# A Mamba block and a six-layer local-attention transformer on one core: V projected per tile, instead of V and output weights folded into one matrix per head

## The chip, the cores and the metric

One NeuronCore of one Trainium2 chip runs one launch. The metric is device time in microseconds (us), the median of a few executions. The kernel before takes 3925.72 us in the median of three (3923.69 to 3927.97).

## What is computed

The input is x, four sequences of 1024 tokens with 128 features, in float32. It goes through a bidirectional Mamba block and then through six transformer layers. The change lies in the attention of these layers; cut to that:

```python
x = x + ffn_ref(layernorm(x))        # the six layers below
for i in range(6):
    x = attn_layer(shift_tokens(x)) + x
    x = ffn_layer(shift_tokens(x)) + x

def attn_layer(x, Wqkv, qs, ksc, Wo):          # 16 heads of 64
    q, k, v = split(x @ Wqkv)                  # each 1024 wide
    q = rotary(l2norm(q) * qs); k = rotary(l2norm(k) * ksc)
    # windows of 32 queries see their own 32 keys and the 32 before
    sim = 8.0 * einsum('bhwie,bhwje->bhwij', q, k2)
    out = einsum('bhwij,bhwje->bhwie', softmax(mask(sim)), v2)
    return out @ Wo
```

## The kernel before

The Mamba block runs first, to about 1120 us. The transformer then works on tiles of 128 tokens (4 windows): 32 tiles a layer, 192 in all, and on chunks of 4 tiles (512 tokens) for the feed-forward part, 48 in all. Activations lie features on partitions (`xa`, `xb`).

A tile passes these stages. `round` (ACT) and `rest` (POOL) split x into a high and a low part; `project0` and `project1` (PE, L1043) multiply it by the weights of q and of k, 3 matmuls of 128x512 for each of two banks (high by high, low by high, high by low), so 12 a tile. ACT squares, DVE and POOL apply rotary tables and norms, `head_turn0..3` (PE, L1054) transpose q and k, four transposes each, and ACT copies them out (L1230). `score` (L1078, L1093) makes 64 small matmuls (16 heads, 4 windows; 64 rows of the array, 32 weight columns, 64 keys streamed) on top of two for the mask. `find_max` (DVE), `exponent` (ACT), `sum_probs` and `invert_sum` (DVE), `normalise_probs` (POOL, L1550) are the softmax, and `turn_probs` (DVE, L1414) transposes the probabilities in blocks of 32x32, which leaves the keys of each window on its own 32 partitions.

V is never formed. Once a layer `fold0` and `fold1` (PE, L1023) multiply each head's V weights by its output weights to a 128x128 matrix, which ACT copies to `w_vo` (`copy_folded`, L1190). Per tile `row_turn` (L1065) transposes x itself, once as it is and once 32 tokens back, `copy_rows` (ACT, L1237) copies both, `mix` (L1105) weights these rows with the probabilities of all 16 heads (8 matmuls of 32 rows by 128 columns, 512 streamed; the windows' four 32-row groups of the array side by side, each into a bank of its own), ACT copies the four banks (`copy_mixed0..3`, L1255), and `output` (L1116) sums over the 16 heads with `w_vo`:

```python
for place_h in range(HEADS):
    last = pe.matmul(bank[:, 0:P], w_vo[:, l % 2, head_at(place_h), :], mixed[:, odd, place_h, :],
                     start=place_h == 0, stop=place_h == HEADS - 1)
```

`add_output` (DVE) adds it to x. The feed-forward stages are `mean`, `variance`, `gate0..2`, `value0..2` (L1141) and `ff_output` (L1154).

Each engine runs its stages in an order written out in a table (`PE_ORDER`, `ACT_ORDER`, `DVE_ORDER`, `POOL_ORDER`): an entry (lag, which, name) stands for the stage of tile `which` of the chunk `lag` rounds back, and `sequence` unrolls it over the 48 chunks. `engine_sequences` puts in the stages that come once a layer. An engine waits on semaphores at the head of a stage, and everything behind it in the table waits too. Four PSUM banks (`turn_banks`) are taken in turn by the stages whose results are copied out; a stage waits until the reader of the bank's last use is done. SP issues weight loads only, when `copy_rows` of certain tiles is done.

## Time and profile before

| | us |
|---|---|
| median of 3 runs | 3925.72 (3923.69 to 3927.97) |
| span of the profiled execution | 3921.5 |
| PE busy | 3707.5 (95%) |
| DVE busy | 3319.6 (85%) |
| POOL busy | 3241.5 (83%) |
| ACT busy | 2915.4 (74%) |

The span is the time from the first to the last instruction of one profiled execution; that execution's own device time is not recorded separately, and its span stands 4.2 us under the median of the runs. PE is TensorE, PEld its weight loads, which run beside its matmuls. A matmul in float32 is recorded as two, each with a weight load; one in fp32r, and a transpose, as one. Busy time is a union: overlapping records count once, so a group's busy time over its number of stages is the price of a stage, while its mean ns holds the latency too.

### The profile page before, as it was taken

To read this page: it belongs to the slowest core of one execution; us is meant where nothing else is said; L and a number is where in the kernel's file an instruction comes from. 1 tells how busy PE (TensorE), PEld (TensorE's weight loads), DVE (VectorE), ACT (ScalarE), POOL (GpSimd) and SP (SyncE) were. 2 spreads that over 40 slices of the span, in tenths; PEclk is the share of its full clock that TensorE was granted. 3 is DMA by queue.
4 is the path that set the end of the run, shared out by engine and by line. 5 is a ranking of instruction groups with operands and counts; after the bars stand their busy time and mean duration, and the time that the engine had idled before them with its cause. 6 is when DMAs were issued, how large, how long until landed. Compare 5 with 4: busy or idle time off the path is not lost.

```text
span 3921.5 us, 110568 instructions
## 1 busy us (share of the span) xinstructions
PE 3707.5 (95%) x43392; PEld 2518.5 (64%) x43392; DVE 3319.6 (85%) x3407; ACT 2915.4 (74%) x6890; POOL 3241.5 (83%) x2370
## 2 busy tenths in 40 slices
PE   7889989988789999999999999999999999999997
PEld 2333333333377777777777777777767777777775
DVE  4999999999688888888888887888878888788885
ACT  7555445553388887888888887888878888888885
POOL 3888888888698888888888888888888888888883
PEclk8999998998899999999999999999999999999999
DMA  1221222212100000000000000000000000000001
GB/s 68 73 76 70 76 71 75 76 71 83 50 16 2 16 3 2 17 2 16 3 6 13 2 16 2 6 13 3 16 2 6 13 2 16 2 6 2 2 3 44
DMA packets 31567, 102.12 MB, mean 26 GB/s; under 512 B 4676, under 2 KB 6600, under 8 KB 30928
## 3 DMA queue, kind: packets, MB, share of 16 engines
q1 hardware_dynamic: 31056, 95.05, 7.0%
q8 instruction: 352, 5.77, 0.6%
q14 instruction: 159, 1.30, 0.1%
HBM read 90.32 MB, written 4.72 MB: 24 GB/s over the span
## 4 chain that ended last, share of the span: by engine, by line
PE 68%; issue 2%; ACT 2%; DVE 0%; POOL 0%; POOLq 0%; ACTq 0%; DVEq 0%
PE ps L1116 17%; PE ps L1043 13%; PE ps L1105 9%; PE ps L1054 8%; PE ps L1093 7%; PE ps L1141 5%; PE ps L1154 3%; PE ps L1078 2%; PE ps L1065 1%; PE ps L1123 1%; PE ps L1129 1%; ACT prob L1246 0%; PE ps L1023 0%; ACT mixed L1255 0%; ACT w_qk L1175 0%
## 5 line engine op out<-in xcount | busy, mean ns | idle before, releaser
L1521 POOL TENSOR_TENSOR resid<-resid,sq 128x1024 f32<-128x1024 f32 x384 | 910.8, 2377 | 3.4 <-DVE sq L1376 2.9
L626 POOL TENSOR_TENSOR read<-state,c_row 128x1024 f32<-128x1024 f32 x256 | 719.8, 2831 | 153.9 <-DVE state L588 84.9
L1543 POOL TENSOR_TENSOR resid<-resid,rnorm 128x1024 f32<-128x1024 f32 x384 | 725.0, 1904 | 18.1 <-POOL rnorm L1535 0.4
L1116 PE MATMUL ps<-mixed,w_vo 128*128 128x128 f32 x6144 | 720.7, 276 | 3.0 <-ACT mixed L1255 2.8
L1116 PEld LDWEIGHTS ps<-mixed,w_vo 128*128 128x128 f32 x6144 | 711.5, 193 | 12.9 <-issue 4.6
L1043 PE MATMUL ps<-w_qk,xs_parts 128*128 128x512 f32 x2304 | 634.6, 411 | 35.4 <-issue 18.1
L1246 ACT ACTIVATE prob<-ps,stat 128x64 f32<-128x64 f32 x3072 | 653.5, 385 | 0.7 <-DVE stat L1396 0.5
L1376 DVE TENSOR_TENSOR sq<-ps,rope_l 128x1024 f32<-128x1024 f32 x384 | 462.4, 1204 | 101.5 <-ACT sq L1208 101.2
L393 PE MATMUL mamba_ps<-read,ident 128*128 128x512 f32 x1024 | 509.6, 638 | 15.4 <-POOL read L626 15.4
L1389 DVE TENSOR_TENSOR resid<-ps,rope_l 128x1024 f32<-128x1024 f32 x384 | 464.3, 1209 | 66.9 <-ACT sq L1208 59.7
L1043 PEld LDWEIGHTS ps<-w_qk,xs_parts 128*128 128x128 f32 x2304 | 412.4, 191 | 148.6 <-issue 73.8
L1550 POOL TENSOR_TENSOR prob<-prob,stat 128x1024 f32<-128x1024 f32 x192 | 366.1, 1907 | 165.3 <-DVE stat L1407 165.3
L1208 ACT ACTIVATE sq<-ps 128x1024 f32<-128x1024 f32 x384 | 395.7, 1030 | 141.3 <-PE ps L1043 111.8
L1255 ACT COPY mixed<-ps 128x512 f32<-128x512 f32 x768 | 399.5, 602 | 111.8 <-PE ps L1105 111.7
L522 ACT ACTIVATE decay<-dt,neg_a 128x1024 f32<-128x1024 f32 x256 | 280.4, 1143 | 268.1 <-DVE state L588 212.6
L1353 DVE TENSOR_REDUCE ssq<-sq 128x16 f32<-128x1024 f32 x384 | 465.7, 1213 | 6.1 <-ACT sq L1208 1.7
L1054 PE MATMUL ps<-ident,resid 128*128 128x128 f32 x3072 | 414.4, 275 | 13.7 <-ACT w_vo L1190 13.1
L588 DVE TENSOR_TENSOR_SCAN state<-decay,mamba_ps 128x1024 f32<-128x1024 f32 x176 | 396.3, 2274 | 3.7
L1054 PEld LDWEIGHTS ps<-ident,resid 128*128 128x128 f32 x3072 | 351.3, 141 | 74.6 <-issue 60.8
L1105 PE MATMUL ps<-prob_t,rows 32*128 32x512 f32 x3072 | 385.2, 613 | 4.1 <-DVE xb L1424 1.6
L393 PEld LDWEIGHTS mamba_ps<-read,ident 128*128 128x128 f32 x1024 | 196.9, 202 | 283.5 <-issue 247.1
L1230 ACT COPY q_t<-ps 128x512 f32<-128x512 f32 x384 | 230.9, 602 | 127.0 <-PE ps L1054 125.0
(138 smaller groups left out, 5676.8 us busy)
## 6 DMA issues: line engine op xcount, KB each, us to landing
c_row<-c_rows SPq DMA_DIRECT2D x128, 512.0 KB, 3.6
w_stage<-w_qk_hbm SPq DMA_DIRECT2D x12, 512.0 KB, 4.7
vo_stage<-w_v_hbm SPq DMA_DIRECT2D x6, 512.0 KB, 3.7
vo_stage<-w_o_hbm SPq DMA_DIRECT2D x6, 512.0 KB, 4.6
xn<-x_hbm SPq DMA_DIRECT2D x4, 512.0 KB, 6.6
kept<-resid SPq DMA_DIRECT2D x8, 256.0 KB, 4.4
resid<-kept SPq DMA_DIRECT2D x8, 256.0 KB, 4.0
out_hbm<-resid SPq DMA_DIRECT2D x8, 256.0 KB, 2.0
```

The source lines that it names most:

```text
L393: last = pe.matmul(y_ps[h][:, c, :], ident[:, :], read[:, h, g % 2, cols(c)], start=False, stop=n == LAST)
L626: pool.tensor_tensor(read[:, h, g % 2, :], state[:, h, g % 2, :], c_row[:, g % C_AHEAD, :], ALU.mult).then_inc(done[f"rd{h}"], 1)
L1043: last = pe.matmul(ps[:, A + c, :], xs_parts[:, odd, xpart, :], w_qk[:, wpart, cols], start=k == 0, stop=k == 2)
L1054: last = pe.transpose(bank[:, j * P:(j + 1) * P], qk[:, tile % 2, col:col + P], ident[:, :])
L1105: last = pe.matmul(banks[w], rows[rows_w, tile % 2, own, :], prob_t[rows_w, tile % 2, :, own, :], start=own == 0, stop=own == 1)
L1116: last = pe.matmul(bank[:, 0:P], w_vo[:, l % 2, head_at(place_h), :], mixed[:, odd, place_h, :], start=place_h == 0, stop=place_h == HEADS ...
L1246: last = act.activation(prob[:, tile % 2, place_h, :], score_ps[:, place_h, :], ACT.Exp, bias=stat[:, tile % 2, 0, place_h:place_h + 1])
L1353: dve.tensor_reduce(ssq[:, tile % 2, part * HEADS:(part + 1) * HEADS, 0], sq[:, 0, :].rearrange("p (h d) -> p h d", d=HEAD_DIM), AX_X, ALU ...
L1376: dve.tensor_tensor(sq[:, 1 + part, :].rearrange("p (h s d) -> p h s d", s=2, d=HEAD_DIM // 2), swapped, table(part, 1, tile).rearrange("p ...
L1389: dve.tensor_tensor(qk[:, tile % 2, part * INNER:(part + 1) * INNER].rearrange("p (h d) -> p h d", d=HEAD_DIM), heads_ps.rearrange("p (h d ...
L1521: pool.tensor_tensor(qk[:, tile % 2, cols], qk[:, tile % 2, cols], sq[:, 1 + part, :], ALU.add).then_inc(done[f"rotated{part}"], 1)
L1543: pool.tensor_tensor(heads, heads, norms, ALU.mult).then_inc(done[f"normed{part}"], 1)
```

## The change

V is computed for each tile: `projv` makes 6 matmuls of the form of `project`, `copy_v0` and `copy_v1` (ACT) bring it to `values`, and two DMAs on SP (`vshift`) write the rows of 32 tokens back beside it. `turn_probs` transposes into a single `prob_t`, and eight DMAs on SP (`pmove`, 64 KB each) move its rows to `by_key`, in which the 64 keys that a window sees lie on 64 partitions. `mix` becomes 64 small matmuls (8 pairs of heads, 2 kinds of window, 2 halves of the rows, 2 heads of a pair): 64 rows by 64 weight columns, 32 queries streamed. ACT copies two banks instead of four, and `output` sums over 8 pairs of heads with the plain output weights. `fold`, `copy_folded`, `row_turn` and `copy_rows` go. The V weights are split once a layer (`high_v` on ACT, `low_v` on POOL, 128x1024 each). `xs_parts` has 4 slots instead of 2. All five tables of the transformer are new; in the Mamba part semaphores are merged.

```diff
-    (2, 2, "head_turn2"), (2, 3, "head_turn0"), (2, 3, "head_turn2"), (2, 3, "head_turn3"), (2, 2, "score"),
+    (4, 1, "project1"), (6, None, "variance"), (4, 0, "head_turn1"), (5, 3, "score"), (5, 1, "mix"), (5, 3, "projv"),
...
+SP_ORDER = [
+    (1, 1, "vshift"), (1, 0, "pmove"), (1, 1, "pmove"), (1, 2, "vshift"), (1, 3, "vshift"), (1, 2, "pmove"),
+    (1, 3, "pmove"), (0, 0, "vshift")]
...
+        insert_after(act, ("copy_v1", last), ("high_v", l))
+        insert_at(pool, (name, last + ahead), ("low_v", l))
...
-    several = {"mix": WINDOWS, "fold0": 2, "fold1": 2}
+    several = {"projv": 2, "mix": 2}
...
+            def shift_values(tile):
...
+                after(sp, ("copy_v0", tile), ("copy_v1", tile))
+                if tile >= 2:
+                    after(sp, ("mix", tile - 2))
...
+                sp.dma_start(v_back[WINDOW:P, odd], v[0:P - WINDOW, odd]).then_inc(v_shifted[odd], 16)
+                sp.dma_start(v_back[0:WINDOW, odd], v[P - WINDOW:P, before]).then_inc(v_shifted[odd], 16)
...
+            def move_probs(tile):
+                odd = tile % 2
+                after(sp, ("turn_probs", tile))
+                if tile >= 2:
+                    after(sp, ("mix", tile - 2))
+                for w in range(WINDOWS):
+                    of = prob_t[w * WINDOW:(w + 1) * WINDOW]
+                    for own in range(2):
+                        first = w // 2 * 64 + own * WINDOW
+                        sp.dma_start(by_key[first:first + WINDOW, odd, w % 2], of[:, own]).then_inc(probs_moved[odd], 16)
...
+            def project_v(tile):
...
+                after(pe, ("rest", tile))
...
+                for c in range(2):
+                    for k, (xpart, wpart) in enumerate([(0, 0), (1, 0), (0, 1)]):
+                        last = pe.matmul(banks[c], xs_parts[:, tile % X_RING, xpart, :], w_v[:, wpart, c * BANK:(c + 1) * BANK],
+                                         start=k == 0, stop=k == 2)
...
             def mix(tile):
-                after(pe, ("turn_probs", tile), ("copy_rows", tile))
-                banks = [turn_free("mix", tile, w) for w in range(WINDOWS)]
-                for own in range(2):
-                    for w in range(WINDOWS):
-                        rows_w = slice(w * WINDOW, (w + 1) * WINDOW)
-                        last = pe.matmul(banks[w], rows[rows_w, tile % 2, own, :], prob_t[rows_w, tile % 2, :, own, :],
-                                         start=own == 0, stop=own == 1)
+                after(pe, ("copy_v0", tile), ("copy_v1", tile))
+                shifted_back(pe, tile)
+                moved(pe, tile)
+                banks = [turn_free("mix", tile, r) for r in range(2)]
+                for a in range(PAIRS):
+                    for second, of in enumerate((v_back, v)):
+                        to = slice(64 * a + WINDOW * second, 64 * a + WINDOW * second + WINDOW)
+                        for r in range(2):
+                            keys = slice(64 * r, 64 * r + 64)
+                            for h in range(2):
+                                head = 2 * a + h
+                                last = pe.matmul(banks[r][64 * h:64 * h + 64, to], of[keys, odd, head * HEAD_DIM:(head + 1) * HEAD_DIM],
+                                                 by_key[keys, odd, second, h * PAIRS + a, :], start=True, stop=True)
...
-                for place_h in range(HEADS):
-                    last = pe.matmul(bank[:, 0:P], w_vo[:, l % 2, head_at(place_h), :], mixed[:, odd, place_h, :],
-                                     start=place_h == 0, stop=place_h == HEADS - 1)
+                for a in range(PAIRS):
+                    last = pe.matmul(bank[:, 0:P], w_o[:, l % 2, a, :], mixed[:, odd, a, :], start=a == 0, stop=a == PAIRS - 1)
...
+                    act.copy(v[:, tile % 2, c * BANK:(c + 1) * BANK], turn_bank("projv", tile, c)).then_inc(done[f"copy_v{c}"], 1)
...
-                if tile >= 2:
-                    after(dve, ("mix", tile - 2))
-                dve.transpose(prob_t[:, tile % 2].rearrange("p h o n -> p (h o n)"),
-                              prob[:, tile % 2].rearrange("p h k -> p (h k)")).then_inc(done["turn_probs"], 1)
+                if tile:
+                    moved(dve, tile - 1)
+                dve.transpose(prob_t.rearrange("p o h n -> p h o n"),
+                              prob[:, tile % 2].rearrange("p h (o n) -> p h o n", o=2)).then_inc(done["turn_probs"], 1)
```

Three places of the new order. First PE in the middle of the transformer. Before, a stretch from a `score` to the second `mix` behind it (`ps<-prob_t,rows` is `mix`, `ps<-mixed,w_vo` is `output`, `ps<-ident,xa` is `row_turn`):

```order
L1093 MATMUL ps<-k_t,q_t 32x64 x64
L1105 MATMUL ps<-prob_t,rows 128x512 x8
L1043 MATMUL ps<-w_qk,xs_parts 128x512 x6
L1129 MATMUL ps<-work_ff,ones_mean 128x512
L1065 MATMUL ps<-ident,xa 128x128 x2
L1116 MATMUL ps<-mixed,w_vo 128x128 x16
L1054 MATMUL ps<-ident,resid 128x128 x4
L1043 MATMUL ps<-w_qk,xs_parts 128x512 x6
L1105 MATMUL ps<-prob_t,rows 128x512 x8
```

Now, from the mix of the second tile of a chunk to that of the third (`ps<-by_key,values` is `mix`, `ps<-w_v,xs_parts` is `projv`, the first of them that of the fourth tile, `ps<-hidden,w` is `ff_output`):

```order
L1133 MATMUL ps<-by_key,values 64x32 x64
L1076 MATMUL ps<-w_v,xs_parts 128x512 x6
L1086 MATMUL ps<-ident,resid 128x128 x4
L1063 MATMUL ps<-w_qk,xs_parts 128x512 x6
L1086 MATMUL ps<-ident,resid 128x128 x4
L1181 MATMUL ps<-hidden,w 128x512 x3
L1086 MATMUL ps<-ident,resid 128x128 x4
L1076 MATMUL ps<-w_v,xs_parts 128x512 x6
L1063 MATMUL ps<-w_qk,xs_parts 128x512 x6
L1133 MATMUL ps<-by_key,values 64x32 x64
L1100 MATMUL ps<-sight_hidden,sight_rows 128x512 x2
```

Between the fourth tile's `projv` and the third tile's `mix` stand seven stages: three of 4 transposes, two `project`, one `ff_output` and one `projv`.

Second ACT, at the copies of the fourth tile's V (`values<-ps`), around the same place of the program:

```order
L1283 COPY mixed<-ps 128x8x64 x2
L1265 COPY values<-ps 128x512
L1222 CAST xs_parts<-xa 128x128
L1265 COPY values<-ps 128x512
L1253 COPY q_t<-ps 128x512
L1231 ACTIVATE sq<-ps 128x1024
L1239 ACTIVATE rnorm<-floored 128x32
```

The two copies follow the two of `mixed`, with a cast between them.

Third SP, which had nothing to issue per tile before (`values<-values` is `vshift`, `by_key<-prob_t` is `pmove`):

```order
L995 DMA values<-values 96x1024 [waits mix,copy_v1,copy_v0]
L996 DMA values<-values 32x1024
L995 DMA values<-values 96x1024 [waits mix,copy_v1,copy_v0]
L996 DMA values<-values 32x1024
L1007 DMA by_key<-prob_t 32x512 [waits mix,turn_probs]
L1007 DMA by_key<-prob_t 32x512 x7
```

The moves of the third tile's probabilities stand behind the shifts of the fourth tile's V, which wait for that tile's copies.

## Rows read from the trace of the kernel before

**Rows 1.** The page: span, busy time of each engine.

```profile
span 3921.5 us, 110568 instructions
...
PE 3707.5 (95%) x43392; PEld 2518.5 (64%) x43392; DVE 3319.6 (85%) x3407; ACT 2915.4 (74%) x6890; POOL 3241.5 (83%) x2370
```

**Rows 2.** The view by stretch; columns of its second line.

```profile
core 0: us, PE busy (x) PEld busy (x) DVE busy (x) ACT busy (x) POOL busy (x), PEclk, DMA share, GB/s
0.00:1120.00 1120.00, 968.37 (x2737) 406.01 (x2738) 987.43 (x668) 596.12 (x743) 878.65 (x365) 0.92 0.20 70
1120.00:1200.00 80.00, 76.46 (x1237) 60.09 (x1236) 65.84 (x77) 66.58 (x176) 71.38 (x59) 0.98 0.05 16
1200.00:3800.00 2600.00, 2561.64 (x38205) 1979.20 (x38205) 2191.70 (x2568) 2177.82 (x5784) 2235.91 (x1906) 1.00 0.02 7
3800.00:3921.00 121.00, 101.07 (x1218) 73.20 (x1218) 74.65 (x97) 74.87 (x191) 55.56 (x42) 0.96 0.11 36
```

**Rows 3.** Waits of PE from 1200 to 3800 us: total, times, longest.

```profile
PE ps L1043 <- issue: 18.1, 7, 3.6
PE ps L1054 <- ACT w_vo L1190: 13.1, 10, 1.3
PE ps L1093 <- issue: 3.3, 10, 0.6
PE ps L1065 <- ACT mixed L1255: 1.2, 5, 0.2
```

**Rows 4.** Groups of PE by form: busy, mean ns | idle.

```profile
L1116 PE MATMUL ps<-mixed,w_vo 128*128 128x128 f32 x6144 | 720.7, 276 | 3.0 <-ACT mixed L1255 2.8
L1043 PE MATMUL ps<-w_qk,xs_parts 128*128 128x512 f32 x2304 | 634.6, 411 | 35.4 <-issue 18.1 <-DVE resid L1389 7.8 <-DVE sq L1376 7.8
...
L1054 PE MATMUL ps<-ident,resid 128*128 128x128 f32 x3072 | 414.4, 275 | 13.7 <-ACT w_vo L1190 13.1
L1105 PE MATMUL ps<-prob_t,rows 32*128 32x512 f32 x3072 | 385.2, 613 | 4.1 <-DVE xb L1424 1.6 <-ACT hidden L1297 0.9
...
L1154 PE MATMUL ps<-hidden,w 128*128 128x512 f32 x192 | 91.7, 601 | 3.8 <-DVE hidden L1438 3.8
...
L1065 PE MATMUL ps<-ident,xa 128*128 128x128 f32 x384 | 75.9, 279 | 1.3 <-ACT mixed L1255 1.2
...
L1154 PE MATMUL ps<-hidden,w 85*128 85x512 f32 x96 | 49.4, 595 | 0.0
...
L1023 PE MATMUL ps<-vo_stage 64*128 64x128 f32 x192 | 13.7, 284 | 0.0
```

**Rows 5.** Timeline of PE: start, us, what.

```profile
1606.44 2.00 PE L1105 MATMUL ps<-prob_t,rows 32*128 32x512 f32 x16
...
1608.69 1.48 PE L1093 MATMUL ps<-k_t,q_t 64*32 64x64 f32 x128
...
1230.11 3.73 PE L1116 MATMUL ps<-mixed,w_vo 128*128 128x128 f32 x32
```

**Rows 6.** Timeline of PE's weight loads in the same score.

```profile
1608.69 1.32 PEld L1093 LDWEIGHTS ps<-k_t,q_t 64*32 64x32 f32 x128 [0.23 <-issue]
```

**Rows 7.** Groups of ACT by form.

```profile
L1255 ACT COPY mixed<-ps 128x512 f32<-128x512 f32 x768 | 399.5, 602 | 111.8 <-PE ps L1105 111.7
...
L1237 ACT COPY rows<-ps 128x256 f32<-128x256 f32 x192 | 77.1, 402 | 0.0
...
L1175 ACT CAST w_qk<-w_stage 128x1024 fp32r<-128x1024 f32 x12 | 13.3, 1104 | 0.0
L1190 ACT COPY w_vo<-ps 128x512 f32<-128x512 f32 x24 | 13.0, 607 | 0.0
```

**Rows 8.** Groups of POOL by form, 1120 to 3921 us.

```profile
L1550 POOL TENSOR_TENSOR prob<-prob,stat 128x1024 f32<-128x1024 f32 x189 | 360.4, 1907 | 165.3 <-DVE stat L1407 165.3
...
L1481 POOL TENSOR_TENSOR w_qk<-w_stage,w_qk 128x1024 fp32r<-128x1024 f32 x10 | 23.6, 2363 | 0.0
```

**Rows 9.** Groups of DVE by form, 1120 to 3921 us.

```profile
L1414 DVE STREAM_TRANSPOSE prob_t<-prob 128x1024 f32<-128x1024 f32 x189 | 234.3, 1240 | 73.2 <-POOL prob L1550 71.8
```

**Rows 10.** Timeline of SP's queue: start, us, DMAs issued.

```profile
4.84 0.81 SPq L272 DMA_DIRECT2D packed<-packed_hbm  x1
...
49.53 1.28 SPq L281 DMA_DIRECT2D c_row<-c_rows  x3
```

**Rows 11.** DMA issues: KB each, median us to landing.

```profile
out_hbm<-resid SPq DMA_DIRECT2D x8, 256.0 KB, 2.0
...
c_rows<-x_dbl SPq DMA_DIRECT2D x8, 64.0 KB, 3.1
...
head_scale<-head_scale_hbm SPq DMA_DIRECT2D x6, 64.0 KB, 4.7
```

260 lines of the change are left out of this document (130 added, 130 removed), and 40 rows, old and new, of tables (ACT_ORDER, DVE_ORDER, PE_ORDER, POOL_ORDER).

## The prediction

> **What bounds the kernel now.** I read the view by stretch first [rows 2]. The Mamba part, to about 1120 us, is not touched by the change (its semaphores are merged, its order stands), so its time stays. In the 2600 us from 1200 on PE is busy for 2561.64, or 98.5%, at a granted clock of 1.00, which is the upper of TensorE's two levels, 2.4 GHz; POOL has 86%, DVE and ACT 84%. The waits of PE in that stretch [rows 3] come to 36 us in all. So the transformer is paid in PE time alone, and every microsecond taken from PE is worth one, until another engine is reached. Over the transformer PE is busy 76.46 + 2561.64 + 101.07 = 2739 us, POOL 2363, DVE 2332, ACT 2319, in a stretch of 3921 - 1120 = 2801 us; PE is idle for 62 us of it, 26 of them outside the middle stretch, where the pipeline fills and drains.
>
> The sum is made against the span of the profiled execution, 3921.5 us [rows 1]. The median of the runs lies 4.2 us above it, and differences are applied to the median.
>
> **The change, part by part, on PE.** Prices of a stage are the busy time of its group over the number of stages.
> - `row_turn` goes: -75.9 us [rows 4].
> - `fold` goes: -13.7 us [rows 4]. With it goes the wait of `head_turn` for the copy of its result, -13.1 us [rows 3].
> - `output` has 8 matmuls of the same form instead of 16: half of 720.7 us, -360.4 [rows 4]. A timeline row shows the stage whole: 3.73 us for 32 records [rows 5].
> - `projv` adds 6 matmuls a tile of the form that `project` has 12 of: half of 634.6 us, +317.3 [rows 4].
> - `mix` today costs 385.2 us, 2.0 us a tile [rows 4, 5]. Its successor, 64 matmuls of 64 rows by 64 weight columns with 32 streamed, is in no row. The nearest one is `score`, also 64 matmuls, of 64 rows by 32 weight columns with 64 streamed: 1.48 us [rows 5]. The new mix streams half as much through places of the array twice as large, so 4 fit side by side instead of 8, and its weight loads are twice as wide. If the number of matmuls or the streaming sets the pace, it costs what `score` does, 1.48 us. If the loads do, it costs up to twice that, 2.96: in `score` the loads fill 1.32 of the 1.48 us [rows 6], so I can't exclude them as the pace. I take 2.0 us, a little under the middle and the price of the stage that it replaces; that makes -1 us, with ends of -101 and +183.
>
> Together -75.9 - 13.7 - 360.4 + 317.3 - 1.2 = -134 us of PE work, to 2605, and -13 us of waiting.
>
> **The other engines.** ACT: `copy_rows` goes (-77.1), the copies of `w_vo` go (-13.0), two copies of `mixed` are replaced by two of V in the same form at 602 ns (0), and `high_v` adds six casts at 1104 ns (+7) [rows 7]: 2236 us, 86% of the new PE work. POOL: `low_v`, six times 2363 ns (+14) [rows 8]: 2377, 91%. DVE: `turn_probs` keeps its size at 1240 ns, but writes in pieces of 32 [rows 9]; below, nothing would be saved; above, twice the price would be +238 us. I take no change, since it turns blocks of 32x32 before and after: 2332, 90%. These costs lie beside PE, which still has the most work. But the cover gets thin: POOL waits 165.3 us in front of `normalise_probs` alone [rows 8], which is a chain and not spare time. I add 20 us of new PE idle time for it.
>
> **SP and the DMAs.** Ten DMAs a tile are new. Three issued in a row take 1.28 us, so 0.43 each; one single issue took 0.81 [rows 10]. Ten are 4.3 us of SP in a tile's 13.6 (2605/192): no bound. What they move, 1 MB a tile, is about 77 GB/s; the Mamba part runs at 70 GB/s with the DMA engines 20% busy [rows 2]. The delay matters. The landing of 64 KB took 3.1 us with one source and 4.7 with another, and 256 KB out took 2.0 [rows 11]. The new mix of a tile waits for its eight moves, which wait for `turn_probs`, and the next `turn_probs` waits for the landing as well, since `prob_t` is single. The tightest place is the one that the orders show: the moves of a chunk's third tile stand on SP behind the shifts of the fourth tile's V. From the end of that tile's `projv` the chain is two copies and a cast on ACT (about 1.5 us), ten issues (4.3) and a landing (3.1 to 4.7): 8.9 to 10.5 us. On PE seven stages lie between: three of 4 transposes (414.4/768 = 0.54 each), three of 6 matmuls (1.65 each) and `ff_output` ((91.7 + 49.4)/48 = 2.9), 9.5 us [rows 4]. So it is just covered at the short landing, and I cost it at nothing. If the cover goes, PE stands in `mix` with `score` and everything else queued behind it. At the end of the program one chain isn't covered: eight issues and a landing, 3.4 + 3.1 = 7 us.
>
> **The sum.** 3925.7 - 134 - 13 + 20 + 7 = 3806 us, 3.1% less.
>
> **Rivals.**
> 1. *The weight loads set the pace of `mix`.* For it: they are twice as wide, and there are 128 per tile. Against: in `score` they run partly beside one another. At 2.96 us a tile it is (2.96 - 2.0) x 192 = +184 us, 3990: slower than before. It decides from 3925.7 - 3806 = 120 us, that is 0.62 us a tile, so from 2.62 us on.
> 2. *`mix` is as cheap as `score`.* For it: same number of matmuls, half the streaming. 0.52 x 192 = -100, less what POOL gives back, since its 2377 us are then 95% of 2505: 3706 to 3726, about 3715.
> 3. *PE waits in `mix` for the moved probabilities.* With the long landing 10.5 - 9.5 = 1.0 us once in each of 48 chunks: +48, 3854. Were each issue to take 0.81, it would be 1.5 + 8.1 + 4.7 - 9.5 = 4.8 us a chunk, +230, 4036, but the shorter issue has three in a row behind it.
> 4. *POOL or DVE becomes the bound.* Their work is unchanged while PE's shrinks by 5%. If half of the 134 us is lost again in their chains: +67, 3873. A dearer `turn_probs` would lead here as well.
> 5. *The change doesn't do what it says* on PE: excluded by the orders, which show `output` at 8, `projv` at 6 and `mix` at 64 matmuls.
>
> **Rule and trace.** Beside rival 1: the loads of `score`, 64 of 32 columns on each half of the rows, are done within 1.32 us [rows 6], 21 ns a load. The Trainium skill (TensorE: Matmul & The Clock Gate, section LDWEIGHTS) puts a load at its columns over 1.2 GHz, 27 ns for 32 and 53 ns for 64. By that rule the new mix would take 64 x 53 = 3.4 us a tile on each half, and the sum would come out at about 4075 us, estimated from that page. The trace is on the faster side of that rule, so it moves no chance. The Trainium skill (TensorEngine Tiling (Array Packing), section Instruction Overhead) gives each matmul about 60 cycles however little it streams; at 2.4 GHz that is 25 ns, for 64 matmuls 1.6 us, an estimate from that page that would bring the sum to about 3730 us. The 64 matmuls of `score` took 1.48 us, 23 ns each, which agrees with it, and speaks for rival 2.
>
> **How the numbers follow.** A difference of 0.2%, 8 us, is about what a measurement of this kernel can tell from none. The forecast has 0.42, rival 1 0.13, rival 2 0.18, rival 3 0.13 and rival 4 0.11; 0.03 is left for something not seen. Faster: the forecast, rivals 2 to 4 but for their far ends (0.02), together 0.82. Slower: rival 1 nearly whole, the far end of rival 3 and half of the unseen, 0.14. The rest, 0.04, is same. The range goes from rival 2, 3715, over rivals 3 and 4 to the point where `mix` costs 2.7 us, 3940; it leaves out the slow half of rival 1 and a little at the cheap end, under 2 in 10.
>
> **What would show it.** PE's group of `mix` over 192: 2.0 us (1.5 is rival 2, above 2.6 rival 1). `output` near 360 us, `projv` near 317, PE busy in all near 3707 - 134 = 3574. Waits of PE in the middle of the transformer: some 30 to 50 us, with nothing on a DMA of `by_key`; over 50 us there is rival 3, on ACT's, DVE's or POOL's results rival 4. `turn_probs` at 1240 ns. A mix above 2.6 us, or a wait on the moved probabilities of more than 2.5 us a chunk, makes the prediction wrong.

## The result, and the profile after

The changed kernel takes 4511.1 us (median of 4 runs, 4508.91 to 4514.13) against 3926.84 us of the kernel before, measured on the same chip: a ratio of 1.149, 95% interval 1.1473 to 1.1506. That is 584 us slower where 120 us less was forecast, and far outside the range. The page of the profiled execution, to read against [rows 1]; the two lines at the end are the clock by slices and the DMA queue that carries instructions:

```profile
span 4512.3 us, 150478 instructions
...
PE 3887.2 (86%) x62400; PEld 2789.0 (62%) x62400; DVE 3324.7 (74%) x3407; ACT 2951.2 (65%) x6772; POOL 3262.0 (72%) x2376
...
PEclk8999999989889899989989999998999889999987
...
q8 instruction: 500, 8.19, 0.8%
```

The work of DVE and POOL is what it was, as forecast; ACT has 2951.2 us where the forecast had 2832 (the last part comes back to it). PE has 3887.2 us of work where the forecast had 3574 (+313), and is idle for 4512.3 - 3887.2 = 625 us where it had 3802 - 3574 = 228 (+397); 3802 is the forecast of 3806, less the 4 us by which the span stands under the median. The two together are the whole miss of 710 us of the span. By stretch [rows 2], the Mamba part is unchanged and the transformer is different everywhere:

```profile
0.00:1120.00 1120.00, 962.26 (x2886) 401.70 (x2887) 985.16 (x664) 590.66 (x720) 878.48 (x361) 0.93 0.22 72
...
1200.00:3800.00 2600.00, 2256.24 (x46140) 1845.47 (x46138) 1811.89 (x2118) 1834.35 (x4693) 1862.10 (x1575) 0.91 0.25 66
```

PE is busy for 87% of the stretch instead of 98.5%, and its granted clock is 0.91 instead of 1.00. PE's groups by form, to read against [rows 4]:

```profile
L1063 PE MATMUL ps<-w_qk,xs_parts 128*128 128x512 f32 x2304 | 668.6, 428 | 29.4 <-issue 8.9 <-DVE resid L1417 8.2 <-POOL w_qk L1509 6.7
...
L1086 PE MATMUL ps<-ident,resid 128*128 128x128 f32 x3072 | 480.6, 298 | 12.2 <-issue 6.2 <-POOL resid L1577 5.7
L1133 PE MATMUL ps<-by_key,values 64*64 64x32 f32 x24576 | 480.6, 230 | 341.1 <-issue 320.1 <-DMA by_key<-prob_t 16.9
L1076 PE MATMUL ps<-w_v,xs_parts 128*128 128x512 f32 x1152 | 388.4, 482 | 3.0 <-issue 3.0
L1144 PE MATMUL ps<-mixed,w_o 128*128 128x128 f32 x3072 | 370.0, 277 | 0.0
L1115 PE MATMUL ps<-k_t,q_t 64*32 64x64 f32 x23808 | 319.1, 231 | 78.0 <-issue 78.0
```

The idle time stands in two groups, `mix` (341.1) and `score` (78.0), and almost all of it is "issue": the profile names no engine and no transfer that PE waited for. The waits of the middle stretch [rows 3] say the same:

```profile
PE ps L1133 <- issue: 252.2, 156, 6.0
PE ps L1115 <- issue: 62.0, 53, 2.5
...
PE ps L1133 <- DMA by_key<-prob_t: 2.0, 2, 1.5
```

Not all of that is one thing. 44 of these stops, 49.3 us, stand at the head of the mix of a chunk's third tile, as here:

```profile
1257.31 5.17 SPq L1007 DMA_DIRECT2D by_key<-prob_t  x8
...
1264.19 1.61 PE L1133 MATMUL ps<-by_key,values 64*64 64x32 f32 x97 [1.45 <-issue]
```

The last of the eight moves is issued at 1261.9 us and lands 2.0 us later, and PE starts 0.3 us after that. Each of the 44 ends within 0.5 us of such a landing. They are waits for the moved probabilities that the profile files under "issue". With the 13.5 us that it puts down to the DMA at the same place in the other 4 chunks, all 48 chunks pay there, 62.8 us in all. The stops inside a stage are the larger part: 224 of them, 350 us, of which 266 in `mix` and 84 in both forms of `score`'s matmuls.

The timeline shows where in a stage PE stops. Two pieces, a score and the mix behind it, twice:

```profile
2017.06 1.48 PE L1115 MATMUL ps<-k_t,q_t 64*32 64x64 f32 x128
2018.57 1.55 PE L1133 MATMUL ps<-by_key,values 64*64 64x32 f32 x90
2021.64 1.08 PE L1133 MATMUL ps<-by_key,values 64*64 64x32 f32 x38 [1.51 <-issue]
...
2034.39 1.72 PE L1115 MATMUL ps<-k_t,q_t 64*32 64x64 f32 x128
2036.13 0.55 PE L1133 MATMUL ps<-by_key,values 64*64 64x32 f32 x22
2038.54 2.74 PE L1133 MATMUL ps<-by_key,values 64*64 64x32 f32 x106 [1.86 <-issue]
```

The stop is in the middle of a mix, once after 90 and once after 22 records, where no instruction waits for a semaphore: all of a mix's waits stand ahead of its first matmul. My reading was that PE is short of instructions. Counting supports it: a float32 matmul of this kernel leaves two records and each record has a weight load, so a mix issues 256 instructions, as a score does, where the old mix issued 32. The traces also show the fetches themselves, as packets of the queue that carries instructions: every one of the 224 stops inside a mix or a score of this kernel ends 1.2 to 1.7 us after such a packet has been moved. Run 4 below shows a row of them. The clock by stretch over the same place (stretch and its length, busy times of the five engines, clock, DMA share, GB/s):

```profile
2018.60:2021.60 3.00, 1.52 (x90) 1.41 (x91) 3.00 (x4) 1.54 (x2) 0.68 (x1) 1.00 0.02 5
2021.60:2026.50 4.90, 4.86 (x51) 4.07 (x51) 2.48 (x5) 1.66 (x3) 3.55 (x2) 0.65 0.02 5
2026.50:2031.00 4.50, 4.50 (x33) 4.08 (x32) 4.20 (x5) 4.24 (x13) 0.97 (x4) 1.00 0.23 56
...
2038.50:2044.00 5.50, 5.46 (x113) 4.71 (x113) 2.58 (x4) 1.07 (x2) 3.59 (x2) 0.55 0.02 4
```

Behind both stops the granted clock falls to 0.55 to 0.65, a mixture of full and half speed (2.4 and 1.2 GHz), for some 5 us in which PE is fully busy, and comes back. So these two stops cost twice: once themselves, and again in the work behind them.

The theories that the experiments had to tell apart: **B**, two stages of 256 instructions in a row use up PE's instructions faster than they come; **A**, the instructions come late because their transfers stand behind the changed kernel's 200 MB of new DMAs; **M**, the small matmuls themselves are slow, whatever stands around them.

### The profile page after: what moved, and what is told of

It reads as the page before. It is cut to its first block, busy times and chain, and to the rows that moved or that the text cites. A ratio compares the mean times of both kernels' runs of the same rounds, so it can differ in the third digit from the quotient of the medians.

```text
span 4512.3 us, 150478 instructions
## 1 busy us (share of the span) xinstructions
PE 3887.2 (86%) x62400; PEld 2789.0 (62%) x62400; DVE 3324.7 (74%) x3407; ACT 2951.2 (65%) x6772; POOL 3262.0 (72%) x2376
## 4 chain that ended last, share of the span: by engine, by line
PE 63%; issue 10%; POOL 2%; ACT 1%; SPq 1%; DMA 0%; DVE 0%; DVEq 0%; ACTq 0%; POOLq 0%
PE ps L1063 12%; PE ps L1133 10%; PE ps L1086 8%; PE ps L1076 8%; PE ps L1144 7%; PE ps L1115 7%; PE ps L1168 5%; PE ps L1181 3%; PE ps L1100 1%; PE ps L1150 1%; PE ps L1156 1%; SPq L1007 1%; POOL resid L1577 0%; POOL resid L1555 0%; ACT prob L1274 0%
## 5 line engine op out<-in xcount | busy, mean ns | idle before, releaser
L625 POOL TENSOR_TENSOR read<-state,c_row 128x1024 f32<-128x1024 f32 x256 | 719.9, 2832 | 154.4 <-DVE state L587 85.0
L1133 PE MATMUL ps<-by_key,values 64*64 64x32 f32 x24576 | 480.6, 230 | 341.1 <-issue 320.1
L1063 PE MATMUL ps<-w_qk,xs_parts 128*128 128x512 f32 x2304 | 668.6, 428 | 29.4 <-issue 8.9
L1133 PEld LDWEIGHTS ps<-by_key,values 64*64 64x64 f32 x24576 | 448.1, 146 | 393.3 <-issue 383.5
L1063 PEld LDWEIGHTS ps<-w_qk,xs_parts 128*128 128x128 f32 x2304 | 454.2, 207 | 126.4 <-issue 34.8
L1563 POOL TENSOR_TENSOR newton<-floored,rnorm 128x32 f32<-128x32 f32 x192 | 49.0, 255 | 660.6 <-ACT rnorm L1241 660.3
L1283 ACT COPY mixed<-ps 128x512 f32<-128x512 f32 x384 | 207.3, 595 | 484.9 <-PE ps L1133 484.9
L1086 PEld LDWEIGHTS ps<-ident,resid 128*128 128x128 f32 x3072 | 415.2, 156 | 137.6 <-issue 64.1
L1086 PE MATMUL ps<-ident,resid 128*128 128x128 f32 x3072 | 480.6, 298 | 12.2 <-issue 6.2
L1115 PE MATMUL ps<-k_t,q_t 64*32 64x64 f32 (+1 forms) x24576 | 319.6, 231 | 84.2 <-issue 84.2
L1076 PE MATMUL ps<-w_v,xs_parts 128*128 128x512 f32 x1152 | 388.4, 482 | 3.0 <-issue 3.0
```

The source lines that it names most:

```text
L625: pool.tensor_tensor(read[:, h, g % 2, :], state[:, h, g % 2, :], c_row[:, g % C_AHEAD, :], ALU.mult).then_inc(done[f"rd{h}"], 1)
L1063: last = pe.matmul(ps[:, A + c, :], xs_parts[:, tile % X_RING, xpart, :], w_qk[:, wpart, cols], start=k == 0, stop=k == 2)
L1076: last = pe.matmul(banks[c], xs_parts[:, tile % X_RING, xpart, :], w_v[:, wpart, c * BANK:(c + 1) * BANK], start=k == 0, stop=k == 2)
L1086: last = pe.transpose(bank[:, j * P:(j + 1) * P], qk[:, tile % 2, col:col + P], ident[:, :])
L1115: last = pe.matmul(ps[w * WINDOW:(w + 1) * WINDOW, S + h, first:(a + 1) * 2 * WINDOW], q_t[rows_h, odd, a, w * WINDOW:(w + 1) * WINDOW], k ...
L1133: last = pe.matmul(banks[r][64 * h:64 * h + 64, to], of[keys, odd, head * HEAD_DIM:(head + 1) * HEAD_DIM], by_key[keys, odd, second, h * P ...
```

## The experiments

All ratios are against runs of the kernel before on the same chip, with 95% intervals. "Gaps" is the idle time on "issue" in `mix` and `score` together, by PE's groups, the waits at the head of a mix with it; "inside" is the time of the stops inside these stages, without those.

**1. No DMAs.** The ten moves of a tile are issued for the first two tiles only; later tiles mix stale probabilities and V.

```diff
             def move_probs(tile):
...
+                if tile >= 2:
+                    return
```

> The changed kernel, with the ten DMAs of a tile (shifts of V, moves of the probabilities) issued for the first two tiles only; all later tiles multiply stale probabilities and stale shifted V, so the output isn't the reference's. PE's order and instructions are the same. Theory A (instruction fetch waits behind these DMAs): the gaps inside mix vanish, the granted clock returns to 1.00 in the transformer, 3790 to 3850 us. Theory B (burst of instructions alone): gaps stay, over 4350 us.

4302.89 us, 1.0967 (1.0887 to 1.1048), in neither theory's range. Gaps 305 us instead of 398, clock 0.938 instead of 0.914.

```profile
L1137 PE MATMUL ps<-by_key,values 64*64 64x32 f32 x24576 | 450.2, 223 | 239.2 <-issue 229.7 <-DVE xa L1485 2.8 <-ACT k_t L1257 1.5
```

So 208 of the 584 us go with the DMAs, and 376 us are there without them: A is a part, and not the main one. In the profiles PE is idle for 103 us less and works 99.5 us less. The waits at the head of a mix, 66 us with those named as the DMA's, are gone, and the stops inside shrink from 350 to 308 us at nearly the same number (224 and 229).

**2. The DMAs alone.** The kernel before with ten DMAs a tile of the same sizes on SP, from SBUF to a scratch in HBM.

> The kernel before, with ten extra DMAs a tile on SP of the sizes of the change (384, 128 and eight of 64 KB), from a constant tile to a scratch in HBM, that nobody waits for but SP. PE's work is the same. Theory A: instructions arrive late behind them, gaps appear in score (one heavy stage a tile instead of two), 3980 to 4150 us. Theory B: no gaps, 3926 to 3940 us.

3932.94 us, 1.0027 (1.0011 to 1.0043). The score's gaps rise from 3.4 to 10.1 us, and that is all:

```profile
L1105 PE MATMUL ps<-k_t,q_t 64*32 64x64 f32 x23808 | 291.1, 226 | 10.3 <-issue 10.1
```

The same traffic costs some 10 us (0.27%) here and 208 in the changed kernel, where PE also waits for what is moved. (The destination differs too, HBM in place of SBUF, so the comparison isn't exact.)

**3. Twice the score, no DMAs.** The kernel before, each of score's matmuls given twice.

```diff
-                for a in range(PAIRS):
+                for a in list(range(PAIRS)) * 2:
```

> The kernel before, with the 64 matmuls of score issued twice in a row (scores doubled, so another output), which adds 256 records a tile right behind the 256 of score, and no DMA. PE's work grows by 1.3 to 1.5 us a tile, 250 to 290 us. Theory A: no gaps without data DMAs, 4180 to 4220 us. Theory B: gaps inside score as in the changed kernel, and a lower clock, 4350 to 4550 us.

4616.64 us, 1.1767 (1.1677 to 1.1857): +690 us for 192 x 1.48 = 284 us of matmuls, more than B's own range (4350 to 4550). A timeline row pair shows B with no DMA and no new form of matmul:

```profile
2013.71 1.83 PE L1093 MATMUL ps<-k_t,q_t 64*32 64x64 f32 x165
2017.14 1.12 PE L1093 MATMUL ps<-k_t,q_t 64*32 64x64 f32 x91 [1.60 <-issue]
```

The page gives the size of what is fetched. The queue of instructions has 544 packets instead of 352; the edit adds 24576 records and as many loads, and 49152 / 192 = 256 instructions a packet. 8.91 MB / 544 is 16 KB, so 64 bytes each. The Trainium skill (Perfetto Trace Analysis, section Per-instruction lifecycle, The 4-stage abstract model) calls instructions 64 bytes long, and the trace agrees.

**4. Four times the score,** to see the pace at which PE goes once its stock is used up.

> Kernel before with every tile's score made of its matmuls four times in a row into the same outputs (the same values are written four times; no transfer is added but the instructions themselves, no order moved). It puts 1024 instructions of PE, matmuls and weight loads, in a row. Theory of fetched instructions: after the instructions at hand are used up PE goes at the pace at which they come, so the last half of each stage shows a steady rate, one stop for each few hundred instructions: with 17 us of added stage at 1.83 us for 165 records gapless the stage would be 512 records in 6 us; by the theory it takes 8 to 12 us. The total is 4616 (score twice) plus 128 tiles times 2 layers... that is 384 tiles in all times 2 more scores of 2.3 to 4 us each: 6000 to 7500 us. Theory M: 512 records run at 1.48 us for 128 to the end, and the total is about 3926 plus 192 tiles times 3 scores times 1.48, 4780 us.

6301.35 us, 1.6066 (1.6028 to 1.6103). A score of this kernel:

```profile
2626.16 2.02 PE L1093 MATMUL ps<-k_t,q_t 64*32 64x64 f32 x183
2630.38 1.47 PE L1093 MATMUL ps<-k_t,q_t 64*32 64x64 f32 x128 [2.20 <-issue]
2633.85 2.04 PE L1093 MATMUL ps<-k_t,q_t 64*32 64x64 f32 x128 [2.00 <-issue]
2637.60 1.34 PE L1093 MATMUL ps<-k_t,q_t 64*32 64x64 f32 x73 [1.71 <-issue]
```

After 183 records the stage falls into a step: 128 records, that is 256 instructions, one packet, then a stop, and the starts are 3.47 and 3.75 us apart. So PE takes in one packet in 3.47 to 3.75 us and uses one up in 1.48 us of score or 2.07 us of mix. The stage took 12.8 us where 512 records at full pace take 5.9, a little over the 8 to 12 expected.

The view of the DMAs from 2620 to 2640 us, in 40 slices of 0.5 us, shows the packets (the 16 is one of another queue):

```profile
GB/s 0 0 0 0 0 0 0 0 16 0 0 0 0 0 0 33 0 0 0 0 0 0 33 0 0 0 0 0 0 33 0 0 0 0 0 0 0 33 0 0
...
q8 instruction: 4, 0.07, 1.5%
```

They begin at 2627.79, 2631.43, 2634.90 and 2638.70 us, and PE goes on 2.4 to 2.7 us after each of the first three. All 566 stops of this trace inside a score end 1.2 to 1.6 us after a packet has been moved. A packet itself is moved in 1.1 us on average and the DMA share of the stage is 0.02, so it is the delay of a fetch and not the rate of the DMA engines that makes the step of 3.5 us. This shows B directly, since no data DMAs were added.

**5. The same work, mixes moved away from scores.** In the changed kernel, three of the four mixes of a chunk, with their copies and `projv`, go behind a later `project0` in PE's and ACT's orders.

> The changed kernel, with three of the four mixes of a chunk moved behind the next project0 (their copies on ACT and the projv that depends on them with them), so that they no longer stand directly behind score. Theory A (PE runs out of instructions because their fetch waits behind SP's data DMAs, wherever the heavy stages stand): 4400 to 4530 us, little better than 4511. Theory B (two stages of 256 records each in a row want instructions faster than an undisturbed fetch brings them): three of four places are mended, so 4050 to 4200 us, and the idle time inside mix falls from 341 us to about 100.

4603.48 us, 1.1733 (1.1661 to 1.1806): slower, a miss for the total that B expected. The part that B is about went as it said: gaps fall from 398 to 166 us. But the edit by hand opened other waits, 97.6 us on ACT's copies in `mix` and 66.7 us on DVE in `project` the largest; over all of PE's groups the waits on ACT and DVE grow by some 265 us. With them the sum closes: PE is idle for 77 us more than in the changed kernel and works 8 us more. A gapless mix is seen here, next to what it costs:

```profile
2043.21 2.07 PE L1112 MATMUL ps<-by_key,values 64*64 64x32 f32 x128
...
L1112 PE MATMUL ps<-by_key,values 64*64 64x32 f32 x24576 | 467.0, 231 | 226.9 <-issue 119.3 <-ACT k_t L1232 97.6 <-DMA by_key<-prob_t 8.7
```

**6. Fewer instructions in the mix, same DMAs.** 32 matmuls of 64 columns in place of 64 of 32.

```diff
-                for a in range(PAIRS):
+                for a in range(0, PAIRS, 2):
...
-                                                  by_key[keys, odd, second, h * PAIRS + a, :], start=True, stop=True)
+                                                  by_key[keys, odd, second, h * PAIRS + a:h * PAIRS + a + 2, :], start=True, stop=True)
```

> The changed kernel with 32 matmuls in mix instead of 64, each streaming 64 columns instead of 32 (the weights of one head are used for two, so half of the heads' values are wrong): same columns streamed, same DMAs with the same bytes, half of the weight loads and half of the instructions. Theory B: gaps inside mix below 80 us, 3750 to 3900 us. Theory A: gaps stay above 200 us, above 4250 us.

4035.64 us, 1.0291 (1.0267 to 1.0315). The streaming and the bytes moved are unchanged and 475 of 584 us are gone. B had expected still more (3750 to 3900 us, gaps inside `mix` under 80):

```profile
L1133 PE MATMUL ps<-by_key,values 64*64 64x64 f32 x12288 | 250.2, 226 | 207.9 <-issue 173.3 <-DMA by_key<-prob_t 31.1
```

The run doesn't part B from M by itself, since the mix's own busy time fell by 230 us (480.6 to 250.2). The stops inside went from 350 to 194 us.

**7. The mix in bfloat16.** 128 instructions a mix instead of 256, and half the bytes in the moves. POOL writes the rounded probabilities to one buffer, and so waits for the last `turn_probs` too.

```diff
-    prob_t = sb("prob_t", [P, 2, HEADS, WINDOW])
-    by_key = sb("by_key", [P, 2, 2, HEADS, WINDOW])
+    prob_t = sb("prob_t", [P, 2, HEADS, WINDOW], BF16)
+    by_key = sb("by_key", [P, 2, 2, HEADS, WINDOW], BF16)
```

> The changed kernel with V, its shifted copy and the probabilities of mix in bf16 (rounded by the copies of V and by normalise_probs): every matmul of mix is one record with one weight load instead of two, so mix brings 128 instead of 256 instructions at the same count of 64 matmuls, and the moves carry half the bytes. Theory B (PE consumes instructions faster than they are fetched, decided by their number in a row): the gaps inside mix fall from 341 us to below 80, the clock is near 1.00, 3700 to 3850 us. Theory M (the small matmuls themselves, their weight loads or the array's tiles, hold PE up): the gaps stay near 300 us, 4300 us or more. Theory A (fetch behind data DMAs only): their number is unchanged and their bytes halved, 4300 to 4450 us.

3985.57 us, 1.016 (1.0133 to 1.0187), over B's range of 3700 to 3850. It is 50 us under the run before it, with half the bytes and 105 us less busy time in the mix (250.2 to 145.6), so the bytes matter little next to the instructions. PE has 3469.4 us of work, less than the kernel before, and the kernel is still slower: gaps are 247 us.

**8. Less work elsewhere, same small stages.** `projv` with its high parts only (2 matmuls, not 6; V is coarser), on the changed kernel and on run 7.

> The changed kernel, projv with the high parts alone (2 matmuls a tile instead of 6), mix untouched: less PE work by 190 to 210 us, the same 256 instructions of mix behind the 256 of score. Theory B with a supply that refills between heavy stages: the time that falls away was refill time, so the gaps inside mix grow and part of the 200 us is lost: 4350 to 4450 us. If supply weren't the limit, all of it would be gained: 4300 to 4320 us.

4354.0 us, 1.1103 (1.1077 to 1.1129).

> The kernel of the bf16 mix, and projv with the high parts alone (2 matmuls a tile instead of 6; V loses its low parts, which bf16 drops anyway). PE's work falls by another 190 to 210 us, below that of POOL, whose 2377 us in the transformer then bound. Theory B: 3600 to 3750 us, faster than both kernels. Theory A: over 4100 us.

3938.45 us, 1.0043 (1.0028 to 1.0058). The first lies in its range (4350 to 4450), the second is far over its own (3600 to 3750). Two thirds of the group of `projv` are 259 us in the changed kernel (of 388.4) and 220 in run 7 (of 329.9). Leaving them out was worth 157 in the one and 47 in the other. The gaps, which B had expected to grow in the first, fell in both (398 to 318, 247 to 206) and stayed the largest idle item; the busy time of `project` and of the transposes rose instead (668.6 to 711.0 and 480.6 to 503.2 in the first), and in the second a wait of 57 us for `by_key` came up.

**9. The lighter mix with the orders of run 5.**

> Changed kernel with the mix in bfloat16 (V, its shifted copies and the moved probabilities are rounded to bfloat16, one recorded matmul and weight load instead of two) and, in addition, the orders of PE and ScalarE moved so that three of four mixes of a chunk no longer stand right behind a score (mix and its copies go behind a later project). Theory of fetched instructions: the gaps for instructions, 153.6 us in mix and 93.5 in score when only the mix was in bfloat16, fall to a third or less as they did under the same move in float32 (295 to 119), and since less is issued at once the clock rises from .945; against it stand the waits that the move itself opened (some 200 us in the float32 case). Net: 3930 to 4050 us, with gaps for instructions in mix and score together under 100 us. Theory M (the small matmuls themselves): the gaps stay at 245 us together, and the total is over 4100 us.

4176.01 us, 1.0654 (1.063 to 1.0678). Again the gaps fell, 247 to 76 us, and the total missed: 190 us slower than run 7.

```profile
L1044 PE MATMUL ps<-w_qk,xs_parts 128*128 128x512 f32 x2304 | 648.5, 418 | 128.5 <-issue 47.5 <-DVE resid L1398 37.6 <-DVE sq L1385 36.8
...
L1114 PE MATMUL ps<-by_key,values 64*64 64x32 bf16 x12288 | 140.2, 182 | 143.3 <-ACT k_t L1234 97.5 <-issue 34.8 <-DMA by_key<-prob_t 9.4
```

The place of a stage can't be changed by hand for one cause alone; each time some 260 us of new waits on ACT and DVE took the place of the gaps.

**10. Score and mix both in bfloat16.** On top of run 7:

```diff
-    q_t = sb("q_t", [P, 2, PAIRS, P])
-    k_t = sb("k_t", [P, K_RING, PAIRS, P])
+    q_t = sb("q_t", [P, 2, PAIRS, P], BF16)
+    k_t = sb("k_t", [P, K_RING, PAIRS, P], BF16)
```

> Changed kernel with the mix and also the score in bfloat16 (V, its shifted copies, the moved probabilities, and q and k are rounded to bfloat16): 64 recorded matmuls instead of 128 in each of the two stages, so that both together issue what score alone issues in the kernel before; orders and all transfers stay (those of mix have half the bytes). Theory of fetched instructions: the gaps for instructions in score and mix, 247 us with only the mix in bfloat16, fall under 60 us; PE's busy time falls by another 100 to 170 us to about 3330. What the total does then tells whether the rest of the step from 3926 was bound by PE at all: if PE alone sets the pace, it is 3986 minus 190 gap minus 130 work, about 3670 us, and waits for transfers stay small; if, as the run with the lighter output showed (360 us less work on PE, total unchanged), the order of the transformer stands at some 3900 us through ScalarE, VectorE and POOL whatever PE has, it is 3850 to 3930 us with PE waiting for those engines by 200 us and more. Theory M (small matmuls are slow in themselves) leaves gaps of 150 us and more for instructions and a total over 3950 us.

3786.69 us, 0.9644 (0.9627 to 0.9662): faster than both kernels. Score and mix together now issue what score alone issued before. Its groups of the two stages:

```profile
L1135 PE MATMUL ps<-by_key,values 64*64 64x32 bf16 x12288 | 137.0, 181 | 171.8 <-DMA by_key<-prob_t 101.7 <-issue 62.7 <-DVE xa L1483 0.9
...
L1117 PE MATMUL ps<-k_t,q_t 64*32 64x64 bf16 x11904 | 133.6, 196 | 24.8 <-issue 24.8
```

The total lies between the two that were weighed (3670, and 3850 to 3930). Gaps are 87 us where under 60 were expected, but 49 of them stand at the head of a mix, just behind a landing of its probabilities; inside the stages 39 are left. The waits for the moved probabilities, my rival 3, are now the larger item: those 49 us and the 101.7 named as the DMA's.

**11. The same edit of q and k on the kernel before and on the changed one.**

> Kernel before with q and k rounded to bfloat16, so that score issues 64 recorded matmuls and 64 weight loads a tile instead of 128 each; nothing else is changed. It tells whether the gain seen with both stages in bfloat16 (3787 us) belongs to the lighter score or to the changed kernel's structure. If PE's work sets the pace of before, 1.48 us of score a tile becomes about 0.75 us: 192 times 0.75 us, 140 us less, about 3785 us, no different from the changed kernel with both light. If instead the transformer of before already stands at its other engines (as the run with the lighter output said, 360 us less on PE and no gain), it stays at 3900 to 3930 us, and then the changed kernel's structure, once its instructions are few, is worth about 3.5%.

3846.8 us, 0.9803 (0.9787 to 0.982), again between the two expected (3785, and 3900 to 3930).

> Changed kernel with q and k rounded to bfloat16 and the mix left in float32: score issues 64 matmuls and 64 weight loads, mix 128 of each, where the changed kernel has 128 and 128, the run with a bfloat16 mix 128 and 64, and the last run 64 and 64. Theory of fetched instructions: what counts is how many instructions stand in a row (score, then mix), so this one should be like the run with the light mix (3986 us) and far from the changed kernel (4511): 3980 to 4150 us, the transfers of mix having their full bytes; gaps for instructions 200 to 280 us, now nearly all in mix, under 30 us in score. If something in the mix itself (its matmuls of 32 columns in float32, or what they read) makes it slow, halving the score changes little: 4300 us or more.

4124.64 us, 1.0509 (1.0485 to 1.0532), gaps 224 us, nearly all in the mix, all as expected by B. Its timeline shows the stock from the other side: 64 and 127 records went through, and the last one had to wait.

```profile
2045.93 0.68 PE L1115 MATMUL ps<-k_t,q_t 64*32 64x64 bf16 x64
2046.72 2.06 PE L1133 MATMUL ps<-by_key,values 64*64 64x32 f32 x127
2051.25 0.19 PE L1133 MATMUL ps<-by_key,values 64*64 64x32 f32 x1 [2.47 <-issue]
```

These runs side by side, in instructions of score and mix in a row (matmul records and loads):

| kernel | score + mix | gaps, us | inside, us | waits for moved probabilities, us | total, us |
|---|---|---|---|---|---|
| changed | 256 + 256 | 398 | 350 | 66 | 4511 |
| changed, score light (11) | 128 + 256 | 224 | 163 | 124 | 4125 |
| changed, mix light (7) | 256 + 128 | 247 | 204 | 66 | 3986 |
| changed, both light (10) | 128 + 128 | 87 | 39 | 151 | 3787 |
| before | 256 + 32 | 3.4 | 4 | none | 3926 |
| before, score light (11) | 128 + 32 | 0 | 0 | none | 3847 |

The waits are those named as the DMA's, and those at the head of a mix under "issue" that end within 0.5 us of a landing of `by_key`. "Inside" counts both forms of the score's matmuls, "gaps" the larger one.

The stops inside follow the count. M falls: the same edit of the score, a stage that the change does not touch, takes 386 of the 584 us from the changed kernel and 79 from the kernel before, though the score's own busy time falls by nearly the same in both (204 and 177 us). At the same count runs 7 and 11 differ by 139 us; in the profiles that is PE's work (3469.4 against 3617.6), while its idle time differs by 10. The changed structure gains 60 us on the old one (3847 to 3787) once both stages are light, with a mix in float32 in the old one.

**12. Half of `output` taken away in the kernel before.** The product is held in the reduced float32 that TensorE takes in one record instead of two, with operands rounded more coarsely.

```diff
-    w_vo = sb("w_vo", [P, 2, HEADS, P])
+    w_vo = sb("w_vo", [P, 2, HEADS, P], F32R)
...
-    mixed = sb("mixed", [P, 2, HEADS, P])
+    mixed = sb("mixed", [P, 2, HEADS, P], F32R)
```

> Kernel before with one change: the product of the output projection (the folded weight of V and output, and the mixed values that it is multiplied with) is held in the reduced form of float32 that TensorE takes in one matmul instead of two, so its operands are rounded more coarsely than before. No order is moved. It takes 16 of 32 recorded matmuls (and as many weight loads) out of each tile's output, 720.7 us of PE by the rows of before, with 3.73 us for 32 recorded matmuls at one width. Theory of fetched instructions (PE stops where its instructions are used up faster than they come): the stage gets lighter in instructions, no new gap for instructions appears in score or mix, and PE's busy time falls by 360 (half of 720.7) to 540 us (a quarter left, if the single matmul is also faster a column). Then PE is no longer alone: POOL with 2363 us of work in the transformer's 2362 us of PE time cannot follow, so the total falls by less: 3550 to 3800 us. Theory that small matmuls themselves are what made the changed kernel slow (M) expects the same fall. A total above 3926 would say that something other than PE sets the transformer's pace already in the kernel before.

3918.44 us, 0.9993 (0.9978 to 1.0008). (The Mamba part, which had worked in `mixed`, works in other buffers.) PE's work fell by 252 us, to 3455.6, where 360 to 540 were expected, and nothing came of it. Both theories had expected a fall; both missed. The idle time moved in front of `project`, `mix` and `score`:

```profile
L1045 PE MATMUL ps<-w_qk,xs_parts 128*128 128x512 f32 x2304 | 663.4, 426 | 191.7 <-DVE resid L1391 118.3 <-DVE sq L1378 46.1 <-POOL w_qk L1483 25.4
...
L1107 PE MATMUL ps<-prob_t,rows 32*128 32x512 f32 x3072 | 402.0, 633 | 62.4 <-ACT rows L1239 34.2 <-ACT hidden L1299 24.8 <-DVE xb L1426 0.8
...
L1095 PE MATMUL ps<-k_t,q_t 64*32 64x64 f32 x23808 | 299.1, 226 | 34.1 <-issue 34.0
```

Against [rows 4] the wait in front of `project` grows from 35.4 to 191.7 us, on DVE's reads of earlier results, that in front of `mix` from 4.1 to 62.4, on ACT, and score's gaps from 3.4 to 34.0. That last number fits B, as there is now less time between two scores in which instructions can come.

## Why the prediction was wrong

**The step that failed** is "the transformer is paid in PE time alone", with "+20 us of new PE idle time" as the only price for PE's idle. PE's time was counted in matmuls; the number of its instructions was read on the page (110568) and never costed. From the code it was countable: 32 instructions a mix became 256, behind a score of 256. What the kernel before couldn't tell is the pace of supply: its longest stretch is one score of 128 records, which just goes through (3.4 us of gaps in all). The packets in the traces, the stops in runs 3 and 4, and runs 10 and 11 beside each other put the cause there: 350 us of stops inside `mix` and `score`, and the clock behind them. No rival of mine named it, and the 0.03 for "something not seen" was far too little for a stage that multiplies its instructions by 8. A second term, put at nothing, failed beside it: the wait for the moved probabilities at the third tile's mix, 62.8 us.

**The clock** was the second part. The forecast took 1.00 as given. It was 0.91, and by my reading that is nearly all of the +313 us of work: stages that the change does not touch became dearer, `project` 634.6 to 668.6, the transposes 414.4 to 480.6, `score` 289.8 to 319.1 [rows 4], 130 us together; `projv` is 71 over its forecast, and `mix` 83 over the 2.07 us a tile that it takes at clock 1.00. No run set the clock by itself.

Term by term:
- `row_turn` and `fold` went, with the wait for `w_vo`: right.
- `output`: forecast 360, measured 370.0. Right.
- `projv`: forecast 317, measured 388.4. The stage takes 1.55 us in a stretch at clock 1.00, as forecast (1.65), and 2.93 right behind a mix that had stopped:

```profile
2029.89 1.55 PE L1076 MATMUL ps<-w_v,xs_parts 128*128 128x512 f32 x6
...
2041.21 2.93 PE L1076 MATMUL ps<-w_v,xs_parts 128*128 128x512 f32 x6
```

- `mix`: taken at 2.0 us a tile, between 1.48 and 2.96. Without a stop and at full clock it is 2.07 us (run 5). Right, so the prices of rival 1 (2.96) and of rival 2 (1.48) both fall. Whether the loads set the pace is open: they are busy for 2.04 of 2.10 us of that gapless mix, and with half the matmuls and the same streaming (run 6) the group falls from 2.50 to 1.30 us a tile, so the streaming does not set it. In the changed kernel the group is 480.6 us, 2.50 a tile, and 1.78 of idle time beside it. My own line said that a mix above 2.6 makes the prediction wrong; the busy time passed that test. The idle time did not pass the test on waits (30 to 50 us in the middle of the transformer; it was 2600 - 2256 = 344), but that line would have named rival 3 or 4 for it, and not the instructions.
- The weight loads, twice as wide, took 1.47 us for 91 in the trace after, at clock 1.00. That is 32 ns a load on each half of the rows. It is under the 53 ns of the rule that I had set beside rival 1, from the Trainium skill (TensorE: Matmul & The Clock Gate, section LDWEIGHTS).
- The 64 matmuls of `score` "at 23 ns each", which I took as agreeing with a floor of 25 ns, are 128 records, 12 ns each. So the agreement was an error of counting, and it should not have spoken for rival 2.
- DMAs: `by_key` landed after 2.0 us in the median, under the 3.1 to 4.7 I took. But an issue took 0.59 us in the median where I took 0.43, and ten of them 6.4 us (1256.04 to 1262.48 at the place shown above) instead of 4.3. That makes the chain 1.5 + 6.4 + 2.0 = 9.9 us where PE's stages were to cover 9.5. So the place that I costed at nothing was not covered: 1.3 us in each of the 48 chunks, 62.8 us, where rival 3 had 1.0 and 48. The 2.0 us that the waits view names in the middle hide it. Rival 3 occurred, beside the failure and not as its main part. With both stages light it is worth 151 us (run 10), within the 48 to 230 that its working gave.
- `turn_probs`: forecast 1240 ns, measured 1236. DVE and POOL as forecast. ACT has 119 us more than its 2832: its new order puts other functions between the three `gelu` of a chunk, so it loads function tables 187 times in the transformer instead of 95, at 1283 ns each. The prediction had that at nothing. PE waits 21.5 us on ACT in all, so it cost nothing here that a row shows. Rival 4 did not occur here.
- "every microsecond taken from PE is worth one": wrong on its own account. Of 252 us less work nothing arrived (run 12); of 130 us less (3707.5 to 3577.5, run 11) 79 did. Where in the order the time is taken decides it. So the forecast of -120 us may have been too good even with instructions free, which no run shows; the kernel before with a light score and the changed one with both stages light differ by 60.

Left open: how much of the lower work in run 1 is the clock alone; why the work of run 9 is 67 us above that of run 7; what sets the delay of a fetch; and which place in the order holds the kernel before at 3920 us in run 12. A search of the orders with the supply of instructions in its costs was not tried.

## What to carry to other kernels

Count the instructions of each stage, weight loads too, and a float32 matmul as two of each, and set them against the time around it: here 150 to 220 records (300 to 440 instructions) went through at full pace, after which 256 more took 3.47 to 3.75 us. Splitting a few large matmuls into many small ones can lower PE's work and still lose several times the gain; a cheaper type that halves the instructions is then worth more than its matmul time says (386 us against 204 for the score). "Idle, issue" in the middle of a stage, each time 1.2 to 1.7 us behind a packet of the instruction queue, is the sign. The same word at the head of a stage can be a wait for a transfer: look for a landing just before its end.

## What the runs showed of the hardware

- The supply: one packet of 256 instructions in 3.47 to 3.75 us with nearly no other traffic (run 4, DMA share 0.02), of which the packet's own move is 1.1 us. With the DMAs 77% busy on data, 1.77 MB in 8 us, and no instruction packet among them, the longest stop of the changed kernel, from 1994.46 us, was 5.96 us. From 1990 to 1998:

```profile
DMA packets 784, 1.77 MB, mean 221 GB/s; under 512 B 199, under 2 KB 396, under 8 KB 784
...
q1 hardware_dynamic: 784, 1.77, 77.3%
```

From 1998 to 2003 us there are two instruction packets, and PE goes on at 2000.42:

```profile
q8 instruction: 2, 0.03, 2.4%
```

```profile
2000.42 2.66 PE L1133 MATMUL ps<-by_key,values 64*64 64x32 f32 x90 [5.96 <-issue]
```

- The clock fell after stops as short as 1.5 us (1.00 to 0.65 above), but not after every one: behind run 3's stop of 1.60 us it stayed at 1.00. What decides between them no run here shows.

```profile
2017.10:2021.00 3.90, 3.86 (x110) 3.51 (x110) 1.39 (x2) 1.62 (x5) 1.23 (x1) 1.00 0.02 4
```

- A small matmul in bfloat16 costs much less than one in float32: 64 of them, 32 columns streamed, took 0.69 us on four places of the array, 11 ns each:

```profile
2016.95 0.69 PE L1135 MATMUL ps<-by_key,values 64*64 64x32 bf16 x64 [0.85 <-issue]
```

The Trainium skill (TensorE: Matmul & The Clock Gate, section Back-to-back issue gap) gives some 60 cycles, about 25 ns, as the floor for up to 64 columns. By that rule 64 take 1.6 us, an estimate from that page; the trace has 0.69, less than half, so the measurement decides: that floor does not hold for these, which lie on four places of the array.
